# Sparse attention plus FP8 linear on one core: row normalisation on ScalarE, near masks shared by two head pairs, q and k stored by three transfers each

## What is computed

```python
q, k, v = xn @ q_w, xn @ k_w, xn @ v_w          # 16 heads of 16 features
scores  = (q * sigmoid(unity)) @ k.T / 4        # per head
allowed = (j % 4 == 0) | (abs(i - j) <= 8)      # strided keys, or near keys
attn    = softmax(where(allowed, scores, -inf)) @ v
out     = x + (attn @ o_w + o_b) + (fp8(xn) @ w8.T + bias)
```

## Time and profile before

| what | us |
|---|---|
| median of 3 runs | 1099.43 (1095.76 to 1100.21) |
| the profiled execution's own time | 1096.05 |
| its span | 1094.2 |
| first stage, to the first attention matmul | about 198 |
| 64 steps, first near score to the start of the last stretch | about 226 to 1040 |
| busy: PE / DVE / ACT / POOL | 1035.1 / 955.5 / 811.2 / 251.9 |

### The profile page before, as it was taken

How to read it: one execution, slowest core, us unless ns; L and a number is a source line. 1 busy time by engine, 2 the same in 40 slices (tenths; PEclk the granted TensorE clock), 3 DMA queues, 4 the chain that set the end, 5 groups by cost and what they waited for, 6 DMA issues and landing times.

```text
span 1094.2 us, 28792 instructions
## 1 busy us (share of the span) xinstructions
PE 1035.1 (95%) x11206; PEld 463.0 (42%) x11207; DVE 955.5 (87%) x1226; ACT 811.2 (74%) x1526; POOL 251.9 (23%) x387
## 2 busy tenths in 40 slices
PE   5899999689999999999999999999999999999898
PEld 2566666333333333333333333333333333333387
DVE  7999998889999999899999999999999899999133
ACT  3444454188888888888888888888888888888700
POOL 2444343111212221212122121222121212212100
PEclk9999999779999999999999999999999999999999
DMA  6567677522332323333332333333243323221166
GB/s 188 188 232 245 232 242 213 177 62 71 93 97 91 88 83 84 108 95 109 88 106 86 101 108 99 102 97 102 84 112 95 106 86 86 86 86 55 46 239 235
DMA packets 166782, 134.15 MB, mean 123 GB/s; under 512 B 70492, under 2 KB 145884, under 8 KB 166636
## 3 DMA queue, kind: packets, MB, share of 16 engines
q1 hardware_dynamic: 163912, 128.06, 38.6%
q10 hardware_dynamic: 2736, 4.26, 1.1%
HBM read 71.13 MB, written 59.84 MB: 120 GB/s over the span
## 4 chain that ended last, share of the span: by engine, by line
PE 60%; DVE 25%; issue 8%; DMA 4%; ACT 3%; DVEq 0%; ACTq 0%
PE ps_attend L1207 16%; PE ps_attend L1135 11%; DVE peak_far L1077 10%; PE ps_attend L1170 9%; PE ps_attend L1214 5%; PE ps_attend L1287 5%; PE ps_attend L1145 4%; DMA sums<-out_rows 3%; PE ps_attend L1181 3%; PE ps_attend L1148 2%; DVE stats L387 2%; PE ps_attend L1188 2%; DVE xn L428 2%; DVE xT_parts L452 2%; DVE base L592 2%
## 5 line engine op out<-in xcount | busy, mean ns | idle before, releaser
L1077 DVE TENSOR_REDUCE peak_far<-ps_attend 128x2 f32<-128x1024 f32 x512 | 608.7, 1221 | 39.3 <-PE ps_attend L1170 29.0
L1018 ACT ACTIVATE probs<-ps_attend 128x512 f32<-128x512 f32 x1024 | 540.9, 598 | 45.9 <-PE ps_attend L1135 42.8
L1207 PE MATMUL ps_attend<-probs,v_op 128*17 128x512 f32 x2048 | 269.8, 599 | 0.5 <-issue 0.5
L1135 PE MATMUL ps_attend<-q_op,k_op 51*128 51x512 f16 x1024 | 254.4, 386 | 4.7 <-ACT probs L1018 3.3
L1170 PE MATMUL ps_attend<-k_op,q_op 48*128 48x512 f16 x1024 | 187.6, 387 | 22.5 <-DVE peak_far L1077 14.1
L1023 ACT ACTIVATE probs<-ps_attend 108x512 f32<-108x512 f32 x256 | 139.0, 594 | 35.8 <-PE ps_attend L1148 35.8
L1135 PEld LDWEIGHTS ps_attend<-q_op,k_op 51*128 51x128 f16 x1024 | 77.4, 93 | 196.2 <-ACT probs L1018 138.3
L884 POOL CAST negmax<-peak 128x16 bf16<-128x16 f32 x64 | 12.7, 198 | 609.2 <-DVE peak L1060 609.2
L1080 DVE TENSOR_REDUCE peak_near<-ps_attend 128x8 f32<-128x864 f32 x128 | 131.0, 1023 | 11.2 <-PE ps_attend L1188 11.1
L875 POOL TENSOR_TENSOR out_rows<-out_rows,share_rows 128x512 f32<-128x512 f32 x64 | 81.5, 1274 | 63.2 <-DMA share_rows<-shares_dram 61.0
L611 PE MATMUL ps_project<-xT_parts,w_parts 128*128 128x512 f16 x384 | 90.7, 387 | 1.0 <-DVE xT_parts L452 0.5
(11 more groups left out here) (91 smaller groups left out, 925.1 us busy)
## 6 DMA issues: line engine op xcount, KB each, us to landing
share_rows<-shares_dram SPq DMA_DIRECT2D x64, 256.0 KB
attn_dram<-out_rows SPq DMA_DIRECT2D x64, 256.0 KB, 5.4
q_dram<-qk_parts SPq DMA_DIRECT2D x96, 128.0 KB
k_dram<-qk_parts SPq DMA_DIRECT2D x96, 128.0 KB
q_op<-q_dram SPq DMA_DIRECT2D x128, 96.0 KB, 2.4
k_op<-k_dram SPq DMA_DIRECT2D x64, 144.0 KB, 3.0
v_dram<-v_sb SPq DMA_DIRECT2D x16, 544.0 KB, 6.8
base<-in_x SPq DMA_DIRECT2D x16, 512.0 KB, 5.3
```

What stands on the lines that cost most here:

```text
L1018: ins = nc.scalar.activation(probs[:, r, h], ps_s[st.bank(kind)], ACT.Exp, scale=undo)
L1077: ins = nc.vector.tensor_reduce(peak_far[:, :, p, tile], banks, AX_X, ALU.max)
L1135: nc.tensor.matmul(bank, k[half(f, KM), keys], q[half(f, KM), p], start=True, stop=True).then_inc(s_ready, 1)
L1207: ins = nc.tensor.matmul(ps_o[h * VW:h * VW + VR], v[:, r, h * VR:(h + 1) * VR], probs[:, r, h], start=(r == 0), stop=False)
```

## The change

Three edits in one:

1. `normalise` moves from DVE to ACT: four activations `Identity(scale * x + bias)` with scale = rstd and bias = shift, both per-row columns in SBUF. ACT runs it for chunk c+2 between the high part of k and the copy of v of chunk c. DVE forms `shift` = -mean * rstd; two of its tiny instructions are fused, so that their number stays at five. `rstd` of a chunk waits until ACT has normalised the chunk before. SP's load three chunks ahead waits for a count of DVE's statistics in place of xn.
2. `score_near` is called for a pair of query tiles in place of a pair of heads: one mask product of 256 columns serves both head pairs of a tile. `near_probs` finds the exponentials in their new places.
3. q and k lie in DRAM as (iteration, pair, half, feature, part, position). The high part of each half of the features is stored by one transfer that writes it to both of its places (256 KB); the low part of both halves by one (256 KB). That makes three transfers for q and three for k in a chunk.

```diff
-                    sp.wait_ge(xn_ready, c + 2)
+                    sp.wait_ge(stat, 7 * (c + 1) + 1)
...
+                    to = dram["qk"[w]][b4:b4 + G, :, :, :, :, cq * CH:(cq + 1) * CH].rearrange(
+                        "(m g) u f r i s -> (g u f r) i m s", m=KC)
+                    if part == LO:
+                        sp.dma_start(to[:, K_ROWS[1][0] if w else Q_ROWS[1][0]], qk_parts[:, k, w, LO]
+                                     ).then_inc(qk_stored[k], 16)
+                        continue
+                    rows = (slice(0, 3, 2), slice(0, 2))[w]
                     for m in range(KC):
-                        for i in (Q_ROWS, K_ROWS)[w][part]:
-                            sp.dma_start(
-                                dram["qk"[w]][bass.ds(b4 + m * G // KC, G // KC), :, :, i, :, cq * CH:(cq + 1) * CH
-                                              ].rearrange("g u f r s -> (g u f) r s"),
-                                qk_parts[:, k, w, part, m]).then_inc(qk_stored[k], 16)
+                        sp.dma_start(to[:, rows, m], qk_parts[:, k, w, HI, m].unsqueeze(1).broadcast_to([P, 2, CH])
+                                     ).then_inc(qk_stored[k], 16)
...
+            def normalise(c):
+                if c > B * CPB - 1:
+                    return
+                act.wait_ge(stat, 7 * c + 7)
+                if c >= 2:
+                    act.wait_ge(t_ready, c - 1)
+                for t in range(TT):
+                    last = nc.scalar.activation(xn[:, c % 2, t], x_in[:, c, t], ACT.Identity, bias=shift[:, t:t + 1],
+                                                scale=rstd[:, t:t + 1])
+                last.then_inc(xn_ready, 1)
...
-                nc.vector.tensor_tensor(newton[:, 2], newton[:, 1], var[:], ALU.mult).then_inc(stat, 1)
+                nc.vector.scalar_tensor_tensor(newton[:, 2], newton[:, 1], -0.5, var[:], ALU.mult, ALU.mult
+                                               ).then_inc(stat, 1)
                 dve.wait_ge(stat, done + 5)
-                nc.vector.tensor_scalar(newton[:, 1], newton[:, 2], -0.5, 1.5, ALU.mult, ALU.add).then_inc(stat, 1)
+                if c > 0:
+                    dve.wait_ge(xn_ready, c)
+                nc.vector.scalar_tensor_tensor(rstd[:], newton[:, 2], 1.5, newton[:, 0], ALU.add, ALU.mult
+                                               ).then_inc(stat, 1)
                 dve.wait_ge(stat, done + 6)
-                nc.vector.tensor_tensor(rstd[:], newton[:, 1], newton[:, 0], ALU.mult).then_inc(stat, 1)
+                nc.vector.scalar_tensor_tensor(shift[:], mv[:, :, 0], -1.0, rstd[:], ALU.mult, ALU.mult
+                                               ).then_inc(stat, 1)
...
-        def score_near(st, p):
+        def score_near(st, i):
...
-            for t in range(TT):
+            for b in range(2):
+                t = 2 * i + b
                 tile = st.queries() * TT + t
+                both, at_mask = slice(b * PAIRS * P, (b + 1) * PAIRS * P), close(tile)
                 for f in range(2):
+                    nc.tensor.matmul(banks[f][0:WIN, both].rearrange("w (p q) -> w p q", p=PAIRS),
+                                     mask_k[half(f), at_mask:at_mask + WIN],
+                                     mask_q[half(f), tile * P:(tile + 1) * P].unsqueeze(1).broadcast_to([KR, PAIRS, P]),
+                                     start=True, stop=False)
+                for p in range(PAIRS):
+                    at = window(p, tile)
+                    for f in range(2):
+                        ins = nc.tensor.matmul(banks[f][0:WIN, (b * PAIRS + p) * P:(b * PAIRS + p + 1) * P],
+                                               k[half(f, KM), at:at + WIN], q[half(f, KM), p, t * P:(t + 1) * P],
+                                               start=False, stop=(p == PAIRS - 1))
...
+        def near_probs(h, t):
+            at = (t % 2 * PAIRS + h // 2) * P
+            return probs[0:WIN, ROUNDS - 1, t // 2 * 2 + h % 2, at:at + P]
```

More of the change, by code:

```diff
@@ L56 @@
 HI, LO = 0, 1
+QK_STORES = 6
 X_RANGE, W_RANGE = 2.0 ** 8, 2.0 ** 13
@@ L85, in load_k @@
     for f, u in pairs:
-        rows = dram["k"][it, u, f].rearrange("i r (c s) -> (i r) c s", c=CPB)
+        rows = dram["k"][it, u, f].rearrange("r i (c s) -> (r i) c s", c=CPB)
         at = WPAD + u * S
@@ L97, in load_q @@
         rows = dram["q"][it, :, f, :, :, queries * CH:(queries + 1) * CH]
-        eng.dma_start(q_op[half(f), slot], rows.rearrange("u i r s -> (i r) u s")).then_inc(loaded, 16)
+        eng.dma_start(q_op[half(f), slot], rows.rearrange("u r i s -> (r i) u s")).then_inc(loaded, 16)
 def part_project(nc, io, dram, keep, ctx):
@@ L126, in part_project @@
         rstd = sb("rstd", [P, TT])
+        shift = sb("shift", [P, TT])
         xn = sb("xn", [P, 2, TT, H])
@@ L333, in body @@
                     if not (isinstance(c, int) and c < 2):
-                        act.wait_ge(qk_stored[k], 16 * 12 * earlier(j, n))
+                        act.wait_ge(qk_stored[k], 16 * QK_STORES * earlier(j, n))
                     nc.scalar.activation(qk_parts[:, k, 0, HI], ps_q, ACT.Copy, scale=PART_SCALES[0]
@@ L412, in deviation @@
                 dve.wait_ge(stat, done + 4)
-                nc.vector.tensor_tensor(newton[:, 2], newton[:, 1], var[:], ALU.mult).then_inc(stat, 1)
+                nc.vector.scalar_tensor_tensor(newton[:, 2], newton[:, 1], -0.5, var[:], ALU.mult, ALU.mult
+                                               ).then_inc(stat, 1)
                 dve.wait_ge(stat, done + 5)
-                nc.vector.tensor_scalar(newton[:, 1], newton[:, 2], -0.5, 1.5, ALU.mult, ALU.add).then_inc(stat, 1)
+                if c > 0:
+                    dve.wait_ge(xn_ready, c)
+                nc.vector.scalar_tensor_tensor(rstd[:], newton[:, 2], 1.5, newton[:, 0], ALU.add, ALU.mult
+                                               ).then_inc(stat, 1)
                 dve.wait_ge(stat, done + 6)
-                nc.vector.tensor_tensor(rstd[:], newton[:, 1], newton[:, 0], ALU.mult).then_inc(stat, 1)
-            def normalise(j, n):
-                c, k = CPB * j + n, n % 2
-                if isinstance(c, int) and c > B * CPB - 1:
-                    return
-                done = 7 * c
-                dve.wait_ge(stat, done + 7)
-                if not (isinstance(c, int) and c < 2):
-                    dve.wait_ge(t_ready, c - 1)
-                for t in range(TT):
-                    last = nc.vector.tensor_scalar(xn[:, k, t], x_in[:, c, t], mv[:, t, 0:1],
-                                                   rstd[:, t:t + 1], ALU.subtract, ALU.mult)
-                last.then_inc(xn_ready, 1)
+                nc.vector.scalar_tensor_tensor(shift[:], mv[:, :, 0], -1.0, rstd[:], ALU.mult, ALU.mult
+                                               ).then_inc(stat, 1)
             def low_part(c, k, w):
@@ L979, in sync_attend @@
         for k in range(2):
-            sp.wait_ge(done["qk_stored"][k], 16 * 12 * B * CPB // 2)
+            sp.wait_ge(done["qk_stored"][k], 16 * QK_STORES * B * CPB // 2)
             sp.wait_ge(done["v_stored"][k], 16 * B * CPB // 2)
@@ L1036, in scalar_attend @@
                 for k in range(2):
-                    act.wait_ge(done["qk_stored"][k], 16 * 12 * B * CPB // 2)
+                    act.wait_ge(done["qk_stored"][k], 16 * QK_STORES * B * CPB // 2)
                     act.wait_ge(done["v_stored"][k], 16 * B * CPB // 2)
@@ L1135, in score_far @@
                 nc.tensor.matmul(bank, k[half(f, KM), keys], q[half(f, KM), p], start=True, stop=True).then_inc(s_ready, 1)
-        def score_near(st, p):
+        def score_near(st, i):
             q, k = q_op[:, st.slot()], k_op[st.parity()]
-            banks = [free_score(st, ("near", 2 * p + f)) for f in range(2)]
-            for t in range(TT):
+            banks = [free_score(st, ("near", 2 * i + f)) for f in range(2)]
+            for b in range(2):
+                t = 2 * i + b
                 tile = st.queries() * TT + t
-                cols, at, at_mask = slice(t * P, (t + 1) * P), window(p, tile), close(tile)
+                both, at_mask = slice(b * PAIRS * P, (b + 1) * PAIRS * P), close(tile)
                 for f in range(2):
-                    nc.tensor.matmul(banks[f][0:WIN, cols], mask_k[half(f), at_mask:at_mask + WIN],
-                                     mask_q[half(f), tile * P:(tile + 1) * P], start=True, stop=False)
-                for f in range(2):
-                    ins = nc.tensor.matmul(banks[f][0:WIN, cols], k[half(f, KM), at:at + WIN], q[half(f, KM), p, cols],
-                                           start=False, stop=True)
-                    if t == TT - 1:
-                        ins.then_inc(s_ready, 1)
+                    nc.tensor.matmul(banks[f][0:WIN, both].rearrange("w (p q) -> w p q", p=PAIRS),
[8 more added lines that the diff above has]
+                                               start=False, stop=(p == PAIRS - 1))
```

(2 more changed lines are left out.)

14 lines of the change are left out of this document (7 added, 7 removed).

## The result

The changed kernel takes 1085.32 us (median of 4 runs, 1084.23 to 1086.84), the kernel before 1099.12 us beside it (4 runs, 1095.76 to 1100.21). The ratio is 0.9884, interval 0.9866 to 0.9901: 1.2% faster. The profiled execution took 1086.01 us with a span of 1084.2 us; that of before 1096.05 with 1094.2, so the two traces differ by 10.0 us, and 3.1 us of the 13.8 between the medians lie in the profiled run of before being a quick one.

What follows compares the result with a forecast made beforehand. DVE was taken to pace the first-stage chunks at 11.17 us, with PE able to do 10.5. 10.0 - 0.3 - 0.4 + 1.0 = 10.3 us won gave 1085.7 to 1089.1, set at 1088 us, range 1081 to 1097.

Steps and rivals of the forecast that it cites:

- Part 1, period: First stage: with the normalisation off DVE, PE's own work sets the chunk, 10.47 us in place of 11.17.
- Part 1, ACT: First stage: four normalising activations take ACT about 1.9 us a chunk, bounds 1.5 and 2.9, within 6.1 us idle.
- Part 1, margin: First stage: DVE's low part of k is done at 2.8 us, PE wants it at 3.5, 0.7 us to spare.
- Part 1, worth: First stage: 1.3 us in the second chunk plus 13 x 0.67 us, 10.0 us won.
- The start: Before the chunk loop: the first two normalisations, exposed and slower on ACT, lose 0 to 1.5 us, taken as 0.3.
- The third set of transposes: Second chunk: of its larger wait of 1.49 us, DVE's 1.30 us go.
- Part 2: Near scores of the steps: merged masks save 5 ns each, 256 times, 1.3 us on PE; 1.0 us taken.
- The rival of 6.3 us: Steps: fewer weight loads let merged masks save 25 ns each, 6.3 us in all, total 1083 us; chance 0.10.
- Part 3: Chunks: six q and k store requests for twelve, same bytes and runs, cost nothing and gain nothing.
- The stores' rival: Chunks: writing one row to two places doubles the stores' price, ACT waits for them, 19 us more, 1118; chance 0.05.
- Identity's table: ACT in the chunks: Identity needs its own table, two loads of 1.283 us a chunk, 1105 us; chance 0.04.
- ACT's dearer adds: First stage: normalised rows come too late for the transposes, each chunk grows 0.6 us, 8 in all, 1108; chance 0.02.

Runs made afterwards that it cites:

- the normalisation alone: The kernel before with only the row normalisation moved from DVE to ACT, masks and stores as before: 1100.86 us, ratio 1.0034.
- an edit that is not in the change: The kernel after with share_rows loaded by four requests of 32 rows, 1081.06 us; or, separately, with DVE's reciprocal of the sums one place later, 1082.32 us.

## Why the prediction came out right, and where it was wrong

The number holds: 1088.0 forecast, 1085.3 measured, range 1081 to 1097, faster. The forecast's mechanism is what happened, DVE under PE. But one step of its working is wrong, and the total is right only because the change held the remedy. That is luck, since the prediction gave this part of the change no worth. The gain itself was put too low, 10.3 us where the medians differ by 13.8.

- **Part 1, period.** 10.47 forecast, 10.42 measured, PE without a wait. PE sets it: 0.87 us less on PE take 0.68 off it. Right.
- **Part 1, ACT.** 1.9 us forecast for the four activations; 2.08 measured, inside the bounds of 1.5 and 2.9. ACT has the time.
- **Part 1, margin.** 0.7 us, for the low part of k. `add_linear` (L602) starts at 115.67, 0.35 us into the chunk, as worked out; the low part of k ends at 118.14 and PE's k starts at 118.79, a margin of 0.65. Two statistics more don't lengthen the chunk.
- **Part 1, worth.** Twelve chunks gave 0.75 us each and one 0.5, in all 9.5 where 13 x 0.67 = 8.7 stood. The start lost 1.4 us (first transposes 0.48 later, the next 0.89 more) where 0.3 stood. The third set of transposes came 3.7 us sooner after the second (14.27 to 10.53 us), where 1.3 stood: only the 1.49 us of the earlier trace rows were counted, not that this whole gap was 3.1 us over the period. After the last transposes 0.2 were won where 0.4 lost stood. In all 9.5 - 1.4 + 3.7 + 0.2 = 12.0 where 9.3 stood.
- **Part 2.** 1.0 us forecast, 2.1 measured. The term was mis-sized: a merged mask, as the prediction counts it (the pair of products for the two banks), saves 17 / 2 = 8.5 ns, not 5, and DVE and ACT hide none of it. The rival of 6.3 us is out.
- **Part 3** is the step that failed. "Cost nothing, gain nothing in the chunks", since "nobody on the path waits for SP". With the old order chunks that begin at 10.42 us don't stay there: from the ninth set of transposes on they average 11.7, and the normalisation alone is 0.34% slower than before. (Why they settle above the 11.17 that the old order does sustain in the kernel before was not tried.) What would have said so was in the trace of the kernel before: 9 arrivals for each store of q and k, never fewer than eight packets in flight from 60 to 100 us, and 6.8 us for v's store to land. The prediction took the share of 0.70 as room, and it is a mean over sixteen engines of which eight have no pause. The Trainium skill's rule on the engines of a transfer, told above from DMA: Bandwidth & Descriptors, would have given 8 for the old stores and 16 for the new.
- **The stores' rival** (1118 us at a doubled price) had the right place, ACT's wait for the stores, and the wrong sign: the change takes load off there. So the sign that it named, a DMA share over 0.8, came true (0.83) and meant the opposite: the same bytes in a shorter chunk on all engines.
- **Late steps.** No term stood for them. By the traces 3.7 us were lost there; by the medians nothing is, and one trace of each kernel doesn't settle it. Some 4 us are had there by an edit that is not in the change.
- **Identity's table.** No table load in the chunks, as forecast. The Trainium skill, ScalarE: Activation LUTs, section Table sets, has identity in every set, and the trace agrees.
- **ACT's dearer adds.** The four activations cover 2.08 us on ACT where DVE's four took 1.30, 0.78 dearer, and the chunk is shorter by 0.75, since ACT had the room. The Trainium skill's rule in ScalarE: Activation LUTs, section Rules for kernel authors, that adds and multiplies are VectorE's, would have made it a loss; the measurement decides against it here.

## What to carry to other kernels

Before you cost a DMA at nothing, ask on how many engines it runs, not only how busy the sixteen are together: count the arrivals at its semaphore, or look at the slowest dimension of both sides after what joins has been joined. A layout in DRAM whose rows join, or a broadcast cut into requests by head, brings the missing engines at no cost in bytes. An edit that takes one engine off the path has to be checked against the next resource under the shorter period: here it is worth 12 us in the first stage or less than nothing, depending on the order of addresses in another part. A small transfer that somebody waits for shouldn't stand behind a large one on few engines.

## What was not expected of the hardware

- A store of 128 KB to DRAM reports 9 times when its DRAM side is (8, 16, 512) and 16 times when it is (128, 512); a gap of one row in 17 undoes it. The price in this kernel is 17.4 us (1104.74 and 1087.32).
- The time that SP takes to issue a store grows when the engines are full: with one and the same order it is 0.59 us in the mean in the kernel before, 0.78 with the normalisation alone and 1.10 with four of the twelve moved to GpSimd. With the new order it is 0.49.
- A request of one source row written to two places costs no more than two requests: the stores of q and k, two in three of this kind, land in 4.7 and 2.7 us at the median for 256 KB, where 128 KB take 3.5 and 2.1.
- Loads of 8 and of 6 KB that usually land in 1.9 and 2.8 us take 5.0 right behind a load of 256 KB that reports 5 times.
- A mask product of 256 columns saves some 4 ns against two of 128 (17 ns for the four of a near score).
